# Gate/up stage of a four-stage kernel: zero points unpacked in column order, so that their spread products read consecutive columns

## The reference, cut to what matters

```python
HID, INTER, BITS, PACK, MAXQ, GROUP = 512, 1376, 4, 8, 15, 128
def _dequant(qweight, scales, qzeros, g_idx):
    shifts = jnp.arange(PACK, dtype=jnp.uint32) * BITS
    w = (qw[:, None, :] >> shifts[None, :, None] & MAXQ).reshape(-1, qweight.shape[1])
    z = ((qz[:, :, None] >> shifts[None, None, :] & MAXQ) + 1).reshape(qzeros.shape[0], -1)
    return (w - z[g_idx]) * scales[g_idx]
Wg, Wu, Wd = (dequant of gate, up: 512 x 1376; of down: 1376 x 512)
h = silu(x @ Wg) * (x @ Wu);  out = h @ Wd
```

## Time and profile before

| | |
|---|---|
| median of 3 runs | 1378.74 us (1378.01 to 1379.72) |
| the profiled execution | 1378.88 us, its span 1377.1 us |
| PE busy over the span | 1292.6 us (94%) |
| DVE, ACT, POOL busy | 921.6 us (67%), 677.4 us (49%), 550.4 us (40%) |
| mean granted clock of PE | 0.975 of full speed |
| DMA | 57.61 MB, 42 GB/s on average |

### The profile page before, as it was taken

How to read it: one execution, slowest core, us unless ns; L and a number is a source line. 1 busy time by engine, 2 the same in 40 slices (tenths; PEclk the granted TensorE clock), 3 DMA queues, 4 the chain that set the end, 5 groups by cost and what they waited for, 6 DMA issues and landing times. The chain is left out here.

```text
span 1377.1 us, 20772 instructions
## 1 busy us (share of the span) xinstructions
PE 1292.6 (94%) x6262; PEld 1009.9 (73%) x6262; DVE 921.6 (67%) x1762; ACT 677.4 (49%) x1055; POOL 550.4 (40%) x557
## 2 busy tenths in 40 slices
PE   5699999999999999999999999999889999879986
PEld 4577877877887787788788778877666666667764
DVE  5876677667667666766766676677665455368995
ACT  3465565566556556656655665664523322222220
POOL 2245335444533534443453444334532334333330
PEclk9899999999999999999999999999989999999996
DMA  4211011011101101100200110010103222131200
GB/s 150 59 47 33 1 62 34 17 33 47 31 1 62 31 16 32 51 28 1 65 29 16 32 59 19 1 36 1 39 16 107 84 76 80 54 94 29 58 16 23
DMA packets 44248, 57.61 MB, mean 42 GB/s; under 512 B 10182, under 2 KB 21156, under 8 KB 43922
## 3 DMA queue, kind: packets, MB, share of 16 engines
q1 hardware_dynamic: 44178, 56.84, 13.5%
HBM read 49.87 MB, written 6.96 MB: 41 GB/s over the span
## 5 line engine op out<-in xcount | busy, mean ns | idle before, releaser
L413 POOL TENSOR_TENSOR x_w<-xs,head_g 128x512 f32<-128x512 f32 x56 | 58.6, 1047 | 280.2 <-ACT xs L522 255.5
L615 DVE SCALAR_TENSOR_TENSOR conv<-p_tile,conv_taps,conv 128x511 f32<-128x511 f32 x189 | 140.8, 745 | 27.6 <-ACT conv L489 17.3
L432 POOL TENSOR_TENSOR y<-y,x_d 128x512 f32<-128x512 f32 x56 | 72.0, 1285 | 170.7 <-DVE y L754 170.7
L726 DVE TENSOR_TENSOR em<-em,p_gb 128x512 f32<-128x512 f32 x128 | 82.2, 684 | 73.0 <-ACT em L528 73.0
L494 ACT ACTIVATE xbc<-conv 128x512 f32<-128x512 f32 x96 | 60.4, 630 | 134.2 <-DVE conv L623 77.6
L1026 PEld LDWEIGHTS p_y<-x_dt,em 128*128 128x128 f32 x896 | 108.6, 192 | 16.1 <-issue 13.0
L615 DVE SCALAR_TENSOR_TENSOR conv<-p_d,conv_taps,conv 128x511 f32<-128x511 f32 (+2 forms) x99 | 73.9, 747 | 68.9 <-ACT conv L489 65.0
L93 PE MATMUL p_tile<-xn_hi,wc_hi 128*128 128x512 f32 x252 | 110.9, 440 | 2.7 <-DVE halo L619 2.7
L93 PE MATMUL p_gate<-wr_hi,xn_hi 128*128 128x512 f32 x256 | 107.0, 418 | 1.1 <-ACT gate L510 1.1
L1026 PE MATMUL p_y<-x_dt,em 128*128 128x64 f32 x896 | 106.1, 271 | 1.0 <-DVE x_res L643 1.0
L93 PE MATMUL p_y<-wr_hi,zt_hi 128*128 128x512 f32 x256 | 103.4, 404 | 1.6 <-ACT zt_hi L498 1.6
(11 more groups left out here) (336 smaller groups left out, 3301.0 us busy)
## 6 DMA issues: line engine op xcount, KB each, us to landing
w_raw<-w SPq DMA_DIRECT2D x112, 256.0 KB, 2.8
q_words<-q SPq DMA_DIRECT2D x33, 256.0 KB, 2.6
h_ring<-h_lo_rows SPq DMA_DIRECT2D x6, 704.0 KB, 5.0
h_lo_rows<-h_rest SPq DMA_DIRECT2D x11, 256.0 KB, 2.0
x_res<-x SPq DMA_DIRECT2D x8, 256.0 KB, 4.5
out<-out_t SPq DMA_DIRECT2D x8, 256.0 KB, 2.1
h_lo_rows<-h_rest SPq DMA_DIRECT2D x11, 128.0 KB, 1.8
decay_lhs<-cum_parts SPq DMA_DIRECT2D x64, 6.0 KB
```

Of the source, the lines that this page charges most:

```text
L413: pool.tensor_tensor(by_head(x_w[:]), by_head(xs[:, c % 2, :]), heads(DTW, c), ALU.mult)\
L432: pool.tensor_tensor(y[:, c % 2, :], y[:, c % 2, :], x_d[:], ALU.add).then_inc(s_txd, 1)
L615: ve.scalar_tensor_tensor(out=conv[:, s, sh:], in0=p[:, 0:HALF - sh], scalar=conv_w[:, bass.ds(g, 1), j, tap], in1=conv[:, s, sh:], op0=AL ...
L726: ve.tensor_tensor(m, m, gm.unsqueeze(1).broadcast_to([P, HG // 2, P]), ALU.mult)\
```

## The change

The zero points are unpacked so that they come out in the order of the weight's columns. The host repeats each packed word eight times in place, and the shift amounts 0, 4, ..., 28 stand along the free dimension, the same on all partitions. The unpacking becomes two DVE instructions (a shift by a second tensor, then an and with 15) with a semaphore between them. The tables become plain [4, 2816] and [10, 512], and the spread products read 128 or 512 consecutive columns.

```diff
-    q_index_i = sb("qi_words", [P, NGI + NGD + 1], I32)
+    q_index_i = sb("qi_words", [P, NGI + NGD + PACK], I32)
...
-            ve.tensor_scalar(q_zero4, q_zero, q_shift, 15, ALU.logical_shift_right, ALU.bitwise_and)\
-                .then_inc(s_q_ve, 1)
+            words, one_in_pack = (a.rearrange("p (n i) -> p n i", i=PACK) for a in (q_zero, q_zero4))
+            ve.tensor_tensor(one_in_pack, words, q_shift.unsqueeze(1).broadcast_to([P, (NSC + NSD) // PACK, PACK]),
+                             ALU.logical_shift_right).then_inc(s_q_z, 1)
+            ve.wait_ge(s_q_z, 1)
+            ve.tensor_scalar(q_zero4, q_zero4, 15, None, ALU.bitwise_and).then_inc(s_q_ve, 1)
...
-    zp_gu = sb("zp_gu", [GU, 8, 2 * NI // 8], BF16)
-    zp_d = sb("zp_d", [P, 8, D // 8], BF16)
+    zp_gu = sb("zp_gu", [GU, 2 * NI], BF16)
+    zp_d = sb("zp_d", [P, D], BF16)
...
-        sp.dma_start(zp_gu[:], q_prep["zp_gu"].rearrange("p n -> (p n)").rearrange("(i g n) -> g i n", i=8, g=GU))\
+        sp.dma_start(zp_gu[:], q_prep["zp_gu"].rearrange("p n -> (p n)").rearrange("(g n) -> g n", g=GU))\
...
-        sp.dma_start(zp_d[0:GD, :, :], q_prep["zp_d"].rearrange("p n -> (p n)").rearrange("(i g n) -> g i n", i=8, g=GD))\
+        sp.dma_start(zp_d[0:GD, :], q_prep["zp_d"].rearrange("p n -> (p n)").rearrange("(g n) -> g n", g=GD))\
...
-            pe.matmul(p_z[slot][:], hot_d[:, rows_t], zp_d[:].rearrange("g i n -> g n i"), start=True, stop=True)
+            pe.matmul(p_z[slot][:], hot_d[:, rows_t], zp_d[:], start=True, stop=True)
...
-        words = zp_gu[:, :, bass.ds(m * (NI // 8) + t * (P // 8), P // 8)].rearrange("g i n -> g n i")
+        words = zp_gu[:, cols]
...
-    io["q_zeros"] = np.tile(np.concatenate([a.reshape(P // 8, -1) for a in zeros], axis=1), (8, 1))
+    io["q_zeros"] = np.concatenate([np.repeat(a, PACK, axis=1).reshape(P, -1) for a in zeros], axis=1)
...
-    io["z_shift"] = (4 * (np.arange(P) // (P // 8))).astype(np.int32).reshape(P, 1)
+    io["z_shift"] = np.tile(4 * np.arange(PACK, dtype=np.int32), (P, 1))
```

More of the change, by code:

```diff
@@ L60 @@
 NI = NT * P
+PACK = 8
 NSC = 2 * GU * NI // P
@@ L184, in mixer @@
     s_split_dt = sem("s_split_dt")
-    s_q_in, s_q_ve, s_q_out = sem("s_q_in"), sem("s_q_ve"), sem("s_q_out")
+    s_q_in, s_q_z, s_q_ve, s_q_out = sem("s_q_in"), sem("s_q_z"), sem("s_q_ve"), sem("s_q_out")
     l2_st, l2_var, l2_rs, l2_xn, l2_tr, l2_hi, l2_lo = (
@@ L295, in mixer @@
     q_index = q_index_i[:, 0:NGI + NGD]
-    q_shift = q_index_i[:, NGI + NGD:NGI + NGD + 1]
+    q_shift = q_index_i[:, NGI + NGD:NGI + NGD + PACK]
     def sync(sp):
```

## The result

| | before | after |
|---|---|---|
| median | 1379.23 us (1378.01 to 1380.74, 4 runs) | 1357.31 us (1356.96 to 1359.74, 4 runs) |
| ratio | | 0.984, 95% interval 0.9828 to 0.9852 |
| profiled execution | 1378.88 us, span 1377.1 us | 1357.26 us, span 1355.5 us |

The forecast was 1358.0 us, range 1354.6 to 1362.0. One of the 17 executions of the kernel before that stand beside the second group of experiments took 3210 us, for a reason that no trace shows; the median of that group is 1379.3 us with it and 1379.2 without.

What follows compares the result with a forecast made beforehand. PE was taken as the bound in the gate/up stage, slowed by stepped zero-point reads. From 1378.88 us, minus 19.5 (blocks) and 1.6 (clock), plus 0.3 (preparation), gives 1358.1, or 1358.0 against the median; range 1354.6 to 1362.0.

Steps and rivals of the forecast that it cites:

- Price of a slow block: Gate/up stage, PE's zero-point spread: each block gives back 0.63 us when its columns are read consecutively, bounds 0.62 to 0.72.
- 31 blocks on the path: Gate/up stage: of 33 zero-point blocks, 31 lie on PE's path, together giving 19.5 us.
- spreads (0,0) and (0,1): First two spreads, from 1015.8 us: gain nothing because DVE is late there; bound 1.3 us if PE were late.
- Nothing takes the wait over: Steady tiles: no other engine or load becomes the limit; the tile shrinks from 14.84 to 12.9 us.
- the 4.2 us in hand: Gate block's rounded weights: ready 5.5 us before their product, 4.2 us after two intervening spreads shorten.
- The clock stretch at 1045.3: Start of the stage: PE's second half-speed stretch goes, giving 1.6 us; rival that it stays, 1359.6 us, chance 30%.
- slow reads made PE look idle: Before 1045.3 us: two back-to-back spreads with 1.7 us of slow reads make busy PE seem idle, halving its clock.
- The preparation: In small_operands: one added DVE instruction and a wait for its end delay PE by 0.3 us, bounds 0 to 0.6.
- Moved buffers, costed at 0: Mixer: a buffer ahead grows by 28 bytes and shifts the others, at no cost.
- Rival "weights bound the short matmuls": Gate/up spreads: loading 128 x 128 one-hot weights sets the pace, 0.11 us per matmul; 1362.0 us, chance 6%.
- Slower, by the clock: Steady part: new half-speed stretches cost 1.6 us each; change loses from 12, at 14 takes 1380.8 us; chance 1%.

Runs made afterwards that it cites:

- the second group of experiments: Runs timed beside the kernel before, unchanged: first run with two slow gate/up spreads, moved buffers, two kernels with several steps; the kernel before took 1379.29 us (17 runs).
- The part kernels (20 and 11 blocks): Changed kernel with only the gate and up tables read in consecutive columns, 1364.69 us, or only the down table, 1371.50 us; the other keeps the old step.
- the kernel with both tables strided: Changed kernel with its new preparation and plain tables, but the spread products read both zero-point tables with the old steps; 1379.61 us, ratio 1.0009.

## Why the prediction was right

- **Price of a slow block** (0.63 us, bounds 0.62 to 0.72). Measured 0.643 from the tile's period; the passage into the spread, 0.10 us, stayed.
- **31 blocks on the path.** The part kernels (20 and 11 blocks) bear the split out. That spreads (0,0) and (0,1) count for nothing is shown by the equal 15.19 us with slow and with short ones.
- **Nothing takes the wait over.** The chain stays on PE; ACT's rounding still waits 1.57 us for its input and none of PE's products waits for it: a gate block is rounded at 1080.24 us and its product begins at 1084.48, so the 4.2 us in hand came out as forecast. Even with the spreads side by side, where 1.2 us were in hand, PE kept its pace.
- **The clock stretch at 1045.3** (1.6 us, taken as going). It went in all five profiles with a fast pair. The step "slow reads made PE look idle" holds as a tendency: five of seven slow pairs brought it, so its mean worth is nearer 1.1 us, an estimate (5/7 of 1.6). That the forecast took all of it, and before's profile had it, is in part luck. By what the reads act on the clock stays open.
- **The preparation** (+0.3 us). Measured +0.27. The table's place in DRAM and the loads: nothing, as the kernel with both tables strided shows.
- **Moved buffers, costed at 0.** This term was mis-sized: 0.4 to 0.6 us, hidden in the scatter of the times. That no read becomes less consecutive was not reason enough.
- **Rival "weights bound the short matmuls".** Four matmuls with their own weights start 55 or 56 ns apart (the second 60 to 67 after the first), zero points and scales alike. These weights are 4 or 12 rows of 128, not the 128 x 128 that the prediction says. By the Trainium skill ("TensorE: Matmul & The Clock Gate", back-to-back issue gap) 81 ns would have been the pace; the trace doesn't agree here.
- **Slower, by the clock.** A slip in the sum: against a gain of 20.8 the change loses from 13 stretches of 1.6 us on, not 12, and 14 of them give 1380.4. No such stretch came: between 1050 and 1150 us of the changed kernel the granted clock is 1.00.

The sum was 20.8 us and the medians differ by 21.9. The profile's own 21.6 contains shares that the forecast knew nothing of, of both signs: +1.8 by a load at the start, +0.6 by the drift, and -2.0 and -1.0 by half-speed stretches around 1008 and 1021 us. That they nearly cancel is luck, and so the last microsecond says nothing for the forecast.

## What to carry to other kernels

Look at the step of the moving operand of small matmuls: with two-byte elements, a step of two cost next to nothing here, three over a third more, four 1.7 times, and from eight elements on a column costs four times as much. It is cheapest to pay for the right order once, where the data is prepared; here a 0.27 us instruction replaced 20 us of slow reads. And once such blocks are short, the way in and out of them is what is left: put them side by side.

## Not expected of the hardware

- A step of four elements of two bytes, two columns to a line of 16 bytes, is not free for PE (96 ns against 56), and nor is three (92 against 67); two nearly is (70 against 67).
- Two slow spreads back to back, with PE busy by the trace in every moment, were followed by a half-speed stretch in five of seven profiles, and two fast ones never in five. It came only where the product ahead of them had run at half speed as well.
- Moving the mixer's buffers by seven words made it about 0.45 us slower in 870, in every profile with the move and in none of the two later ones without.
